# Samples of a row pair by way of a DRAM scratch, with the convolution one round later

## The reference

```python
def _L1_conv_ref(x, w_om, b_om, weight, bias):          # x: normalized, (8, 32, 128, 128)
    om = conv3x3(x, w_om) + b_om                        # 27 values for each pixel
    off = om[:, :18].reshape(-1, 9, 2, Ho, Wo)          # where each of 9 taps looks
    mask = sigmoid(om[:, 18:])
    ys = off[:, :, 0] + tap_y + row;  xs = off[:, :, 1] + tap_x + column
    vals = bilinear_sample(x, ys, xs) * mask[:, None]   # (b, c, 9, y, x): the samples
    return einsum('bckhw,ock->bohw', vals, weight) + bias
x = x + _L0_conv_ref(_gn(x), ...)
x = x + _L1_conv_ref(_gn(x), ...)
```

## Time and profile before

| What | us |
| --- | --- |
| Median of 3 executions | 2575.74 |
| Lowest and highest of them | 2557.75, 2578.82 |
| The profiled execution's own time | 2586.75 |
| Its span | 2584.9 |
| TensorE busy | 1895.4 |
| VectorE busy | 1674.9 |
| ScalarE busy | 1468.7 |
| GpSimd busy | 1253.1 |

### The profile page before, as it was taken

How to read it: one execution, slowest core, us unless ns; L and a number is a source line. 1 busy time by engine, 2 the same in 40 slices (tenths; PEclk the granted TensorE clock), 3 DMA queues, 4 the chain that set the end, 5 groups by cost and what they waited for, 6 DMA issues and landing times.

```text
span 2584.9 us, 123141 instructions
## 1 busy us (share of the span) xinstructions
PE 1895.4 (73%) x48729; PEld 1242.9 (48%) x48729; DVE 1674.9 (65%) x2942; ACT 1468.7 (57%) x2476; POOL 1253.1 (48%) x1676
## 2 busy tenths in 40 slices
PE   8553477777777877787778777777777777777784
PEld 3311255555555555454555555554545545455553
DVE  8696276666666666666676656666666666666673
ACT  0013576666666665666665656666656666565662
POOL 0000265555555565555564555555545555555562
PEclk9698598888888898888897988888888889898897
DMA  8046555555555555555555655555555555555563
GB/s 295 17 166 279 153 138 142 141 134 137 140 146 145 140 139 137 141 139 140 135 150 150 158 143 139 136 133 141 134 131 135 142 138 146 136 136 133 135 156 96
DMA packets 328050, 372.89 MB, mean 144 GB/s; under 512 B 45752, under 2 KB 269976, under 8 KB 323480
## 3 DMA queue, kind: packets, MB, share of 16 engines
q1 hardware_dynamic: 327576, 365.40, 52.5%
HBM read 142.25 MB, written 71.97 MB: 83 GB/s over the span
## 4 chain that ended last, share of the span: by engine, by line
SPq 40%; PE 23%; issue 14%; DVE 10%; DMA 9%; DVEq 2%; ACT 1%; POOL 1%; POOLq 0%; ACTq 0%
SPq L479 30%; PE pM L1074 7%; DMA v<-big 7%; PE pV L1049 6%; PE pE L1025 4%; PE pM L1061 4%; DVE big L768 2%; SPq L438 2%; SPq L427 2%; DVE big L811 2%; DVE big L791 1%; SPq L417 1%; SPq L461 1%; SPq L466 1%; PE pM L1094 1%
## 5 line engine op out<-in xcount | busy, mean ns | idle before, releaser
L552 POOL TENSOR_TENSOR halves<-prod,halves 128x300 f16<-128x300 f32 x768 | 601.2, 783 | 914.3 <-DVE halves L806 659.9
L811 DVE COPY big<-pE 128x768 f32<-128x768 f32 x768 | 726.8, 946 | 443.1 <-PE pE L1025 438.3
L647 ACT ACTIVATE big<-pE 128x768 f32<-128x768 f32 x768 | 632.2, 823 | 531.1 <-PE pE L1025 524.8
L1049 PE MATMUL pV<-big 128*32 128x144 f32 x16384 | 743.1, 311 | 38.4 <-issue 29.0
L1025 PE MATMUL pE<-big,sel_s 32*128 32x64 f16 (+1 forms) x24576 | 456.1, 212 | 333.5 <-DVE big L811 201.2
L1025 PEld LDWEIGHTS pE<-big,sel_s 32*128 32x128 f16 x24576 | 355.7, 97 | 597.8 <-issue 562.5
L543 POOL TENSOR_TENSOR prod<-big 128x300 f32<-128x300 f32 x768 | 564.3, 735 | 91.6
L1049 PEld LDWEIGHTS pV<-big 128*32 128x32 f32 x16384 | 469.9, 116 | 115.7 <-issue 58.6
L791 DVE STREAM_TRANSPOSE big<-halves 128x384 f32<-128x384 f32 x768 | 437.9, 570 | 22.1 <-POOL halves L552 2.1
L661 ACT ACTIVATE big<-pV 128x432 f32<-128x432 f32 (+1 forms) x640 | 306.5, 479 | 134.2 <-PE pV L1049 83.0
L1074 PE MATMUL pM<-v,wc 96*32 96x256 f32 x3072 | 246.1, 462 | 174.1 <-DMA v<-big 174.0
(11 more groups left out here) (73 smaller groups left out, 1064.0 us busy)
## 6 DMA issues: line engine op xcount, KB each, us to landing
v<-big SPq DMA_DIRECT2D x1536, 96.0 KB
big<-xh_scratch SPq DMA_DIRECT2D x384, 136.0 KB, 2.8
tr_scratch<-share SPq DMA_DIRECT2D x134, 144.0 KB
big<-tr_scratch SPq DMA_DIRECT2D x134, 144.0 KB, 2.6
win<-xh_scratch SPq DMA_DIRECT2D x134, 136.0 KB, 2.9
xh_scratch<-stg SPq DMA_DIRECT2D x32, 544.0 KB, 2.7
big<-in_x SPq DMA_DIRECT2D x16, 1024.0 KB, 16.9
x_scratch<-big SPq DMA_DIRECT2D x16, 1024.0 KB, 3.9
```

What stands on the lines that cost most here:

```text
L552: nc.gpsimd.tensor_tensor(half[:, rn % 2, :, 0:SQ, 1], prod[:, rn % 2, :, :], half[:, rn % 2, :, 0:SQ, 0], ALU.subtract).then_inc(low_done, 1)
L647: nc.scalar.activation(*expanded(1 - q, r, 0), ACT.Copy).then_inc(e_act, 1)
L811: nc.vector.tensor_copy(*expanded(1 - q, r, 1)).then_inc(e_dve, 1)
L1049: last = mm(pV[r % 2][b * C:(b + 1) * C, o:o + TAPC], XT[:, t * P + b * C:t * P + (b + 1) * C], av[:, b * NT + t, :], start=True, stop=True)
```

## The change

The twelve moves of a pair go away. In their place SyncE's step N ends with one store of the whole `VS[q]` into a new DRAM scratch with two halves, and step N + 1 has, after the window pair, a new function `load_samples`: it waits for the convolution before and for the store, and then loads v2 in three transfers, for each ky one of 32 partitions x 4 images x 3072 bytes. The convolution and outs move from round 4 to round 5 on every engine that takes part. The first copy into `VS[q]` waits for the store (`vs_st`) of two pairs before, in place of the moves.

```diff
@@ -54,13 +54,13 @@
 VGROUPS = [(0, 1, 2), (3, 4, 5), (6, 7, 8), (9, 10, 11), (12, 13), (14, 15)]
 TAPC = TAPS * TILE_R * TILE_C
 
-OM_AT, OMT_AT, SIG_AT, ABS_AT, RELU_AT, CONV_AT = 0, 1, 2, 3, 4, 4
+OM_AT, OMT_AT, SIG_AT, ABS_AT, RELU_AT, CONV_AT = 0, 1, 2, 3, 4, 5
 TURN_AT = 2
 HATS_AT = 1
 HIGH_ACT = (1, 0, 1, 0, 1, 0)
 V_ACT = (1, 1, 1, 0, 1, 1)
 UNROLL = 4
-NV2 = IPG * KS
+NV2 = KS
 BN_EPS = 1e-5
 XCH = 512
 NXC = HW // XCH
@@ -99,6 +99,7 @@
         x1_d = nc.dram_tensor("x1_scratch", (g_count * P, HW), fp32, kind="Internal").ap()
         xh_d = nc.dram_tensor("xh_scratch", (g_count * P, PADR * PADC), fp32, kind="Internal").ap()
         tr_d = nc.dram_tensor("tr_scratch", (g_count * GPAIRS * POS, P), fp32, kind="Internal").ap()
+        vs_d = nc.dram_tensor("vs_scratch", (2 * P, KS * KS * PX), fp32, kind="Internal").ap()
         xt_d = nc.dram_tensor("xt_scratch", (g_count * IPG * HW, C), fp32, kind="Internal").ap()
 
 
@@ -238,6 +239,7 @@
 
         win_ld = [sem(f"win_ld{i}") for i in range(SLOTS)]
         wino_ld = [sem(f"wino_ld{i}") for i in range(2)]
+        vs_st = sem("vs_st")
         v2_ld = sem("v2_ld")
         x1_ld = [sem(f"x1_ld{i}") for i in range(2)]
         out_st = [sem(f"out_st{i}") for i in range(2)]
@@ -438,6 +440,17 @@
                     sp.dma_start(wino[ky * C:(ky + 1) * C, q, :, :, :].rearrange("c b r x -> c b (r x)"),
                                  rows.rearrange("(b c) n -> c b n", b=IPG)).then_inc(wino_ld[q], 16)
 
+            def load_samples(n, q):
+
+                wait(sp, conv_done, n)
+                sp.nop(nofuse=True)
+                sp.wait_ge(vs_st, (n + 1) * 16)
+                sp.nop(nofuse=True)
+                for ky in range(KS):
+                    taps = vs_d[q * P:(q + 1) * P, ky * KS * PX:(ky + 1) * KS * PX]
+                    sp.dma_start(v2[ky * C:(ky + 1) * C, :, :, :].rearrange("c b k n -> c b (k n)"),
+                                 taps.rearrange("(b c) n -> c b n", b=IPG)).then_inc(v2_ld, 16)
+
             def step(N, phase, on, place):
                 q = phase % 2
                 if isinstance(N, int) and N == -1:
@@ -446,6 +459,8 @@
                     load_rows(N + 2, q, place)
                 if on[-1]:
                     load_pairs(N + 1, (phase + 1) % SLOTS, place)
+                if on[3]:
+                    load_samples(N - 3, 1 - q)
                 if on[1]:
                     sp.wait_ge(turn_st, turned_by(*place(N - 1)) * 16)
                     sp.nop(nofuse=True)
@@ -473,12 +488,8 @@
                 if on[2]:
                     sp.wait_ge(v_act, (N - 1) * VN[1])
                     sp.wait_ge(v_dve, (N - 1) * VN[0])
-                    wait(sp, conv_done, N - 2)
-                    for b in range(IPG):
-                        for ky in range(KS):
-                            sp.dma_start(v2[ky * C:(ky + 1) * C, b, :, :].rearrange("c k n -> c (k n)"),
-                                         VS[q][b * C:(b + 1) * C, ky * KS * PX:(ky + 1) * KS * PX]) \
-                                .then_inc(v2_ld, 16)
+                    sp.nop(nofuse=True)
+                    sp.dma_start(vs_d[q * P:(q + 1) * P, :], VS[q]).then_inc(vs_st, 16)
             steps(sp, step)
             for q in range(2):
                 sp.wait_ge(out_st[q], 16 * (NPAIR // 2) * g_count)
@@ -657,7 +668,7 @@
                     if on[2] and V_ACT[r]:
                         act.wait_ge(v_done, (N - 2) * len(VGROUPS) + (r + 1))
                         if v_count(1, r) == 0:
-                            wait(act, v2_ld, (N - 3) * (16 * NV2))
+                            wait(act, vs_st, (N - 3) * 16)
                         nc.scalar.activation(*evacuate(q, r), ACT.Copy).then_inc(v_act, 1)
                     if on[0] and r == TURN_AT:
                         g, local = place(N)
@@ -826,7 +837,7 @@
                     if on[2] and not V_ACT[r]:
                         dve.wait_ge(v_done, (N - 2) * len(VGROUPS) + (r + 1))
                         if v_count(0, r) == 0:
-                            wait(dve, v2_ld, (N - 3) * (16 * NV2))
+                            wait(dve, vs_st, (N - 3) * 16)
                         nc.vector.tensor_copy(*evacuate(q, r)).then_inc(v_dve, 1)
                     if on[3] and r == CONV_AT:
                         n = N - 3
```

## The result

The changed kernel takes 2960.57 us, the median of 4 executions (2954.75 to 2974.17), against 2577.28 for the kernel before: 1.1503 times as long, 95% interval 1.1419 to 1.1587. That is 383 us lost where 36 were forecast as gained, and beyond the range of 2420 to 2680. The profiled execution has a span of 2953.5 us.

What follows compares the result with a forecast made beforehand. SyncE's twelve move issues per pair were taken to bound the kernel; the new loop, 4.5 + 4.5 (store) + 7.0 (loads) = 16.0 us against 16.37, saves 1.1 us per four pairs, 36 us in all: 2540 us, range 2420 to 2680.

Steps and rivals of the forecast that it cites:

- What bounds the kernel before: SyncE's twelve issues per pair, in a loop of 16.37 us; the engines alone need 14.2 us.
- 4.5 + S + L: New loop per pair: 4.5 us fixed, S the store's landing, L the loads' landing; 16.0 us against 16.37.
- Loads, 7.0: L, the three loads into v2, first issue to last landing: 7.0 us, between 4.9 and 8.4.
- the Trainium skill's port rule: 32 partitions reach 8 of 16 ports at 27.2 GB/s each: loads 7.4 us, sum 16.4, no gain.
- Store, 4.5: S, the 1152 KB store to DRAM until landing: 4.5 us, between 4.2 and 6.0.
- The low clock: At the convolution: a wait of 1.8 us stays under the 3 us at which the lower clock follows.
- Not a bound, but queues get longer: DMA engines: transfers take 12.6 of 17.4 us of a step on each engine, so no bound.
- B: Rival: store and loads land late on shared rings, loop over 17.3 us, about 2790 us; chance 0.20.
- A: Rival: loads run at the full rate, loop 13.6 us, under the engines' 14.2, about 2367 us; chance 0.15.
- The fit named beside it: The Trainium skill's single-transfer fit, 2.0 us plus bytes over 436 GB/s: store and loads at 4.7 us each.
- C: Rival: the stall at the loop's start grows by 1.4 us x 32, no change, about 2585 us; chance 0.18.
- The moved step, at nothing: Convolution and outs from round 4 to round 5: costs nothing, covered by the wait of 1.8 us.

Runs made afterwards that it cites:

- Experiment 12: Kernel before, with the three moves of the last image issued by ScalarE and nine by SyncE: 2391.05 us, ratio 0.9298.
- Experiment 3: Changed kernel with the loads of the samples issued ahead of the row loads and window pair: 2935.20 us, ratio 1.1429.
- experiment 5: Changed kernel with the store ahead of SyncE's wait for outs and the loads ahead of the rows: 2804.46 us, ratio 1.0850.
- experiment 11: Kernel before with its twelve moves, plus a store of VS to the scratch that nobody reads: 2730.73 us, ratio 1.0607.
- 14: Kernel before with nine moves on SyncE, three on ScalarE, plus a store of VS to the scratch that nobody reads: 2591.64 us, ratio 1.0086.
- experiment 10: Changed kernel with one load of the same 1152 KB to 128 partitions in place of three to 32, samples in wrong places: 2629.16 us, ratio 1.0227.
- experiment 13: Changed kernel with the store ahead of the wait for outs and one load to 128 partitions, samples in wrong places: 2553.31 us, ratio 0.9935.
- experiment 8: Changed kernel with convolution and outs back in round 4: 3045.06 us, ratio 1.1787.
- experiment 1: Kernel before with its twelve moves, only convolution and outs one round later: 2584.78 us, ratio 1.0029.
- experiment 6: Changed kernel with the scratch laid out as v2: four stores, one per image, and one load of 96 partitions: 3121.51 us, ratio 1.2103.
- experiment 4: Changed kernel with the store of the samples ahead of SyncE's wait for outs: 2650.57 us, ratio 1.0327.

## Why the prediction was wrong

**What bounds the kernel before: right.** Experiment 12 took the twelve issues off the one queue and got the 14.2 to 15 us for an ordinary interval that I had read off two waits.

**The loop of the changed kernel: right in form, wrong in size.** The legs of the interval shown add up to it to the last hundredth. But 4.5 + S + L was taken as 16.0 and is 19.09 in the interval shown. The terms:

- Loads, 7.0 in the sum, 8.58 measured. The step that failed is "I take 7.0": the queue ahead, 544 KB of rows and window, I had only put into the upper end, though SyncE issues just these between the store and its wait for the store, so that they are always ahead. Experiment 3 prices them at about 1 us. Then the rate: 218 GB/s for 1180 kB is 5.4 us, not 5.0. Some 0.2 us are left. "Their issues cost no more" was wrong too: the three take 1.89 and 2.37 us for 1.35, which is part of the 8.58. The rate from the stretch of the moves (118 GB/s at a share of 0.50) was near; the estimate of 7.4 from the Trainium skill's port rule was nearer. The upper end of 8.4 was not high enough.
- Store, 4.5, measured 5.25, within the bounds. What lies ahead, counted in full where I had halved it, gives 4.9; the rest of the way to 5.25 no run explains.
- The low clock, 0 in the sum. The convolution takes 2.79 us in place of 1.57, and the leg from its start to the end of outs 3.34 for 2.29, 1.05 more. I had read off one row that a wait of 3 us is needed. In the rows after, convolutions of 2.79 us stand behind waits of 1.93 and 1.39 us. The whole trace of the kernel before would have told: over 2.2 us took none of 74 convolutions behind a wait of up to 1 us, 2 of 11 behind 1 to 2 us, 14 of 18 behind 2 to 3, and 24 of 25 behind more. The 2.63 us with a quick convolution in the earlier trace rows was the exception. In the changed kernel the row for 1 to 2 us is 15 of 18, so the forecast's wait of 1.8 us was no safe one.

These three are 1.58 + 0.75 + 1.05 = 3.38 us, less 0.28 for the leg from outs to the store (1.82 for 2.10) and 0.04 for the wake: 3.06 us over 16.03, which is 19.09. The sum would have told it with the right terms.

**"Not a bound, but queues get longer": the step that failed beside the loop.** I divided 12.6 us of work on the DMA engines by a period of 17.4 and stopped there. The work is not spread. It lies in one stretch of 12 us with every engine full, and other things on the rings come later: TensorE's instructions (experiment 5), the regions (experiment 11), the rows (5.4 us to landing for 2.8). Experiments 11 and 14 price the store's bytes alone at 155 and 201 us in kernels where no load waits for them. How much of this the longer loop covers in the changed kernel can't be read off. Its fourth interval, 24.00 us where I had "near 21.6", is longer by TensorE's lower clock and not by stalls.

**Rivals.** B was the one that came: its place (the wait at the convolution) and its slow convolutions are the result's, and S + L was 13.8, over its point of 12.8. Its 2790 us are still 170 short: it gave 6.7 us in four pairs, and it was 11.6. I gave it 0.20, since I held its conditions for mishaps and not for the rule. Its evidence against, "a large store leaves the rings after 4.2 us when it is alone", did not bear on it, for the store is never alone here. A was shown false by experiment 10 for the loads as they are made, and by 13 for its time: even with a loop of 12.7 us the kernel stays at 2553 us, not 2367. The fit named beside it is given on that page of the Trainium skill for transfers issued from GpSimd; these are SyncE's, and the two legs took 5.25 and 8.58 us, not 4.7. C did not come in the changed kernel: its stall at the loop's start, in "issue" 4.72 us before, is 4.44 after. It came in experiments 8, 11 and 14, with 7.4, 6.4 and 6.2 us (5.4 in experiment 12, which 14 starts from).

**The moved step, at nothing: right** for the kernel before (experiment 1, 1.0029). With the scratch it is worth some 84 us to the good (experiment 8), which no step of mine had.

**What stays open.** How the 383 us divide between loop and bytes has no single answer, since each hides the other: removing the store from the loop gives 310, the shorter loads 331, and both together 407 of them (experiment 13), while the bytes alone cost 155 to 201. Unexplained are the rate of experiment 6, the short bursts of the row loads over 218 GB/s, and why the round matters in experiment 8.

## What to carry to other kernels

Before a transfer is called hidden, draw up what is on the rings microsecond by microsecond around it, and not only the mean share: what the issuing queue sends out just before it waits lies in front of what it waits to send, and TensorE stalls for its instructions more often when they are full. A loop of dependences by way of DRAM pays two landings, each of them behind whatever is on the rings; here it helped to take one of them out of the loop (experiment 4). When a mean clock falls, look at TensorE's busy time before its stalls: half of this loss lies there. And a kernel bound by one queue's issues may first be helped by another queue: three of twelve moved to ScalarE gave 7%, six gave a loss.

## What the runs showed of the hardware

- The three loads of v2, 32 partitions each, moved 218 GB/s at a share of 1.00 (1806 to 1811 us of the changed kernel), and landed after the same 6.9 us from the scratch and from the input; the store from 128 partitions moved 360 GB/s (1800.2 to 1803.2 us). Short row loads to 32 partitions reached 266 GB/s.
- TensorE's stalls in "issue" within a group of matmuls end 1.2 to 1.9 us after a 16 KB packet of the instruction queue (145 of 148 in experiment 5). There such a stall of over 1 us follows 71% of the packets that start with the DMA engines full, and 14% of those with a share under 0.4; 16% of all packets in the kernel before.
- The longer the wait before it, the more often a convolution ran at the lower clock (over 2.2 us for 1.57): in the kernel before 2 of 11 after 1 to 2 us, 14 of 18 after 2 to 3. In the changed kernel, with a mean clock of 0.78, 15 of 18 after 1 to 2 us, and 14 of 27 with no wait over 0.3 us. The length of the wait alone does not tell which.
